# Output weights gated in a batch's second group, and the maxima's rows spread to the heads by a transfer

## What is computed

```python
mod = (silu(c) @ wmod).reshape(4, 6, 1, -1)          # sa, ca, ga, sb, cb, gb
ga = (2 * (ga >= 0) - 1) * maximum(abs(ga), 0.25)    # gb likewise
h = layernorm(x) * (1 + ca) + sa
q, k, v = split(h @ W_qkv.T); q, k = rope(q), rope(k)
y = softmax(causal(q @ k.T / sqrt(32))) @ v          # for each head
x = x + ga * (y @ W_o.T)
h = layernorm(x) * (1 + cb) + sb
x = x + gb * moe(h)      # top 2 of 16 by sigmoid(h @ Wg.T + bias), silu(h @ W1) @ W2
```

## Time and profile before

| | |
|---|---|
| median of three runs | 1663.24 us (1660.96 to 1666.24) |
| profiled execution | 1664.53 us, span 1662.6 us |
| TensorE (PE) busy | 1417.6 us, 85% |
| VectorE (DVE) busy | 1252.3 us, 75% |
| ScalarE (ACT) busy | 832.3 us, 50% |
| GpSimd (POOL) busy | 726.1 us, 44% |
| mean granted TensorE clock | 0.939 of full |

### The profile page before, as it was taken

One profiled execution on the slowest core, in us unless ns is written; L12 is line 12 of the kernel. 1 busy time (PEld: TensorE's weight loads), 2 busy tenths in 40 slices (PEclk: granted clock), 3 DMA queues, 4 the chain that ended last, 5 costly groups with the idle time before them and its releaser, 6 DMA issues. The chain is left out here.

```text
span 1662.6 us, 27877 instructions
## 1 busy us (share of the span) xinstructions
PE 1417.6 (85%) x8713; PEld 1008.2 (61%) x8713; DVE 1252.3 (75%) x2928; ACT 832.3 (50%) x1414; POOL 726.1 (44%) x683
## 2 busy tenths in 40 slices
PE   5579998799999889999988999999783999999900
PEld 3556665566566556656655565664341899999800
DVE  3578788687778868777886777888658677777778
ACT  4324557534454753445466434546323566666622
POOL 3244445342434534243443424344524677777500
PEclk9899999999999999999999999999885999999955
DMA  6644453544344353434445353434654555445389
GB/s 218 173 152 153 134 146 89 165 121 153 101 134 137 99 165 120 153 102 133 126 109 165 114 159 94 123 94 140 214 176 154 164 173 182 158 148 169 120 324 370
DMA packets 130098, 254.56 MB, mean 153 GB/s; under 512 B 15792, under 2 KB 67504, under 8 KB 129984
## 3 DMA queue, kind: packets, MB, share of 16 engines
q1 hardware_dynamic: 101888, 177.12, 34.5%
q0 software_dynamic: 13792, 47.72, 8.5%
q10 hardware_dynamic: 14304, 28.32, 5.1%
HBM read 167.34 MB, written 85.75 MB: 152 GB/s over the span
## 5 line engine op out<-in xcount | busy, mean ns | idle before, releaser
L674 ACT ACTIVATE probs<-ring 128x1024 f32<-128x1024 f32 (+3 forms) x384 | 310.2, 811 | 191.6 <-PE ring L528 115.8
L493 PE MATMUL ring<-stack_t 96*128 96x512 f32 (+3 forms) x768 | 296.6, 410 | 26.7 <-DMA stack_t<-stack_dram 23.5
L471 PE MATMUL ring<-w_parts,h_hi 128*128 128x384 f32 x1024 | 273.8, 349 | 9.2 <-DVE neg_max L855 4.0
L858 DVE CUSTOM_DVE_ANT_0 ring<-ring,later_b 128x384 f32<-128x384 f32 (+3 forms) x512 | 247.7, 496 | 31.5 <-PE ring L493 30.3
L493 PEld LDWEIGHTS ring<-stack_t 96*128 96x128 f32 x768 | 141.8, 193 | 181.5 <-issue 66.6
L1155 POOL TENSOR_TENSOR rope_a<-rope_a,rope_b 128x256 f32<-128x256 f32 x128 | 93.2, 728 | 348.6 <-DVE rope_b L928 348.5
L1142 POOL TENSOR_TENSOR prob_sum<-prob_sum,probs 128x1024 f32<-128x1024 f32 (+3 forms) x128 | 226.1, 1766 | 28.8 <-ACT probs L674 27.7
L522 PE MATMUL ring<-stack_t 128*128 128x512 f32 (+3 forms) x768 | 212.0, 358 | 23.0 <-ACT probs L674 11.2
L471 PEld LDWEIGHTS ring<-w_parts,h_hi 128*128 128x128 f32 x1024 | 188.9, 195 | 17.9 <-issue 12.9
L855 DVE TENSOR_REDUCE neg_max<-ring 128x1 f32<-128x512 f32 x256 | 174.9, 683 | 24.8 <-PE ring L493 22.6
L471 PE MATMUL ring<-w_parts,h_lo 128*128 128x384 f32 x512 | 176.2, 344 | 0.0
(11 more groups left out here) (192 smaller groups left out, 2439.3 us busy)
## 6 DMA issues: line engine op xcount, KB each, us to landing
stack_t<-stack_dram SPq DMA_DIRECT2D x384, 128.0 KB, 3.3
stack_dram<-parts SPq DMA_DIRECT2D x64, 512.0 KB, 2.7
w_parts<-w_dram SPq DMA_DIRECT2D x24, 768.0 KB, 6.6
w_sb<-y_dram SPq DMA_DIRECT2D x32, 512.0 KB, 6.7
w_sb<-w SPq DMA_DIRECT2D x22, 512.0 KB, 5.9
x_in<-x SPq DMA_DIRECT2D x32, 256.0 KB, 3.6
x<-x SPq DMA_DIRECT2D x32, 256.0 KB, 3.6
x_dram<-x SPq DMA_DIRECT2D x32, 256.0 KB, 2.4
```

The source lines that it names most:

```text
L471: mm = nc.tensor.matmul(ring[:, BANK[use], 0:384], lhs[:, c, cols], rhs[:, c, :], start=(k == 0), stop=(k == len(products) - 1))
L493: nc.tensor.matmul(ring[:, BANK[use], 0:width], stack_t[0:MROW, i % 2, 0, h, qt * P:qt * P + P], stack_t[0:MROW, i % 2, 1, h, kc * 512:kc ...
L674: nc.scalar.activation(probs[:, step % PROBS, :, q0:QC], ring[:, bank:bank + 2, q0:QC], ACT.Exp)\
L858: nc.vector.tensor_tensor_reduce(ring[:, BANK[use], 0:width], ring[:, BANK[use], 0:width], later_b[:, QC - width:QC], -1.0, 3e38, ALU.add, ...
```

## The change

The reads of the gate row and of the output weights move from steps 0 to 5 of the fourth group to steps 10 to 13 of the second group of the same batch; the modulation rows from step 7 of the fourth to step 15 of the second; the four products on POOL from steps 7, 8, 9, 11 of the fourth to steps 17, 19, 21, 23 of the second. ScalarE copies the maxima's rows for head 0 alone; SyncE waits for that copy and issues a transfer within SBUF from head 0's rows to those of heads 1 to 3, and TensorE waits for the transfer. Besides, two pairs of semaphores on POOL are merged into one each.

```diff
-LOAD_MOD2 = {STEPS * (G * b + G - 1): b for b in range(B)}
-LOAD_W_OUT = {step + 2 + n: (b, n) for step, b in LOAD_MOD2.items() for n in range(G)}
-LOAD_MOD_ROWS = {step + 7: b for step, b in LOAD_MOD2.items()}
-GATE_OUT = {step + at: (b, n) for step, b in LOAD_MOD2.items() for n, at in enumerate((7, 8, 9, 11))}
+LOAD_MOD2 = {STEPS * (G * b + 1) + 10: b for b in range(B)}
+LOAD_W_OUT = {step + n: (b, n) for step, b in LOAD_MOD2.items() for n in range(G)}
+LOAD_MOD_ROWS = {step + 5: b for step, b in LOAD_MOD2.items()}
+GATE_OUT = {step + at: (b, n) for step, b in LOAD_MOD2.items() for n, at in enumerate((7, 9, 11, 13))}
...
+            rows_in = [sem("rows_in0"), sem("rows_in1")]
...
+                    def rows_to_heads(i, half):
+                        rows = stack_t[MROW:MROW + 2 * HG, i % 2, 0, :, half * QC:half * QC + QC].bitcast(f32)
+                        sp.wait_ge(max_in, 2 * i + half + 1)
+                        sp.dma_start(rows[:, 1:HG, :], rows[:, 0:1, :].to_broadcast([2 * HG, HG - 1, QC]))\
+                            .then_inc(rows_in[half], 16)
...
                         if step in STACK_IN:
                             stack_parts(*STACK_IN[step])
+                        if step in MAX_TURN:
+                            rows_to_heads(*MAX_TURN[step])
                         if step in SECOND_STAT:
...
                         if kt == 0 and hp == 0:
-                            pe.wait_ge(max_in, 2 * i + qc + 1)
+                            pe.wait_ge(rows_in[qc], 16 * (i + 1))
...
-                        nc.scalar.copy(stack_t[MROW:MROW + 2 * HG, i % 2, 0, :, half * QC:half * QC + QC],
-                                       row.unsqueeze(1).to_broadcast([2 * HG, HG, QC])).then_inc(max_in, 1)
+                        nc.scalar.copy(stack_t[MROW:MROW + 2 * HG, i % 2, 0, 0, half * QC:half * QC + QC], row)\
+                            .then_inc(max_in, 1)
...
-                            dve.wait_ge(rstd2_ready, u - 1)
+                            dve.wait_ge(rstd2_ready, 2 * (u - 1))
...
-                        dve.wait_ge(rstd2_ready, u + 1)
+                        dve.wait_ge(rstd2_ready, 2 * u + 2)
...
-                            .then_inc(rstd_pow, 1)
-                        pool.wait_ge(rstd_pow, u + 1)
+                            .then_inc(rstd_step, 1)
+                        pool.wait_ge(rstd_step, 2 * u + 2)
```

More of the change, by code:

```diff
@@ L297, in adaln_block @@
             x_in_s = [sem(f"x_in{k}") for k in range(3)]
-            stat_step, rstd_step, rstd_pow, rstd_ready = (
-                sem("stat_step"), sem("rstd_step"), sem("rstd_pow"), sem("rstd_ready"))
+            stat_step, rstd_step, rstd_ready = (
+                sem("stat_step"), sem("rstd_step"), sem("rstd_ready"))
             stat_ready, x_hat_ready, h_scaled = sem("stat_ready"), sem("x_hat_ready"), sem("h_scaled")
@@ L312, in adaln_block @@
             o_ps, x1_ready, res_in = sem("o_ps"), sem("x1_ready"), [sem("res_in0"), sem("res_in1")]
-            stat2_step, stat2_ready, rstd2_step, rstd2_ready = (
-                sem("stat2_step"), sem("stat2_ready"), sem("rstd2_step"), sem("rstd2_ready"))
+            stat2_step, stat2_ready, rstd2_ready = (
+                sem("stat2_step"), sem("stat2_ready"), sem("rstd2_ready"))
             x_hat2, h2_ready = sem("x_hat2"), sem("h2_ready")
@@ L1108, in first_deviation @@
                             .then_inc(rstd_step, 1)
-                        pool.wait_ge(rstd_step, u + 1)
+                        pool.wait_ge(rstd_step, 2 * u + 1)
                         nc.gpsimd.tensor_tensor(rstd[:, u % 2, 1:2], rstd[:, u % 2, 0:1], neg_half[:, :], ALU.pow)\
-                            .then_inc(rstd_pow, 1)
-                        pool.wait_ge(rstd_pow, u + 1)
+                            .then_inc(rstd_step, 1)
+                        pool.wait_ge(rstd_step, 2 * u + 2)
                         nc.gpsimd.tensor_scalar(rstd[:, u % 2, 2:3], mean_var[:, u % 2, 0:1], rstd[:, u % 2, 1:2], -1.0,
@@ L1119, in second_deviation @@
                         nc.gpsimd.tensor_scalar(rstd2[:, u % 2, 0:1], mean_var2[:, u % 2, 1:2], EPS, None, ALU.add)\
-                            .then_inc(rstd2_step, 1)
-                        pool.wait_ge(rstd2_step, u + 1)
+                            .then_inc(rstd2_ready, 1)
+                        pool.wait_ge(rstd2_ready, 2 * u + 1)
                         nc.gpsimd.tensor_tensor(rstd2[:, u % 2, 1:2], rstd2[:, u % 2, 0:1], neg_half[:, :], ALU.pow)\
```

## The result

The changed kernel takes 1652.32 us (median of four runs, 1650.18 to 1653.38) against 1662.37 us for the kernel before, measured beside it: a ratio of 0.9934, 95% interval 0.9914 to 0.9955. A second set of runs, further down, gives 0.9928 (0.9910 to 0.9945). The gain is real, but 10 to 13 us where 27 were forecast; the median lies just above the upper end of the range, 1652. The profiled execution took 1653.06 us, span 1650.1 us.

What follows compares the result with a forecast made beforehand. The prediction took the attention part to be bound by TensorE nearly everywhere, with gains only where it waits or runs at half clock. 10.0 + 13.8 + 4.2 - 1.0 = 27.0 us gave a median of about 1636 us, range 1628 to 1652.

Steps and rivals of the forecast that it cites:

- (a): Last batch: early gated weights remove TensorE's wait before the output projection and its half clock; gain 10.0 us.
- R4: Rival: the residual holds the last batch's projection instead, so no gain there; 1646 us, chance 0.08.
- (b): Fourth groups, batches 0 to 2: TensorE's waits for stacked q/k parts and the half clock behind go; gain 13.8 us.
- R1: Rival: the third pair's stack in the fourth groups stays late; 1650 us, chance 0.17.
- (c): Second groups: the reads and POOL products moved there cost zero, at most 1 us for each batch.
- part 1: Output weights read and gated early, in the second group: gains of 10.0 and 13.8 us.
- small things: Allowance of 1 us for possible small costs, such as the row transfer and delayed expert loads in the last group.
- Part 2: Maxima's rows copied for one head: 1.28 us of ScalarE saved 32 times, worth 4.2 us on the path.
- The four places: Step 3 of three fourth groups and the last group, where the shorter copy saves TensorE waiting: 4.2 us.
- The transfer: SyncE's row transfer, taken to land in 2.7 us: cost 0, up to 5 us in the last group.
- R2: Rival: the row transfer on SyncE's queue delays the stacked parts in 15 groups; 1700 us, chance 0.04.

Runs made afterwards that it cites:

- e5: Changed kernel with four-head row copies, no row transfer, and early output weights in the last batch only: 1649.33 us, ratio 0.9928.
- e1: Changed kernel with only the early weight reads and gating; rows copied for all four heads, no transfer: 1642.42 us, ratio 0.9867.
- e6: Changed kernel with four-head row copies, no transfer, and early output weights in batches 0 to 2 only: 1653.25 us, ratio 0.9940.
- e7: Kernel before with only the two modulation rows read early, at step 15 of the second group: 1654.94 us, ratio 0.9956.
- e11: e5 with the modulation rows of all batches also read in the second group: 1643.33 us, ratio 0.9884.
- e4: Changed kernel with the copy for all four heads put back and the row transfer kept: 1642.09 us, ratio 0.9859.
- e3: Changed kernel with VectorE's probability sum waiting for POOL's reciprocal root in steps with a layer norm: 1639.01 us, ratio 0.9846.
- e9: Changed kernel, unaltered, measured again against the kernel before: 1650.48 us, ratio 0.9928.
- e12: e3 measured once more, beside e10: 1641.82 us, ratio 0.9873.
- e8: e2 with VectorE's sum also waiting for POOL's reciprocal root, as in e3: 1655.23 us, ratio 0.9959.
- e10: e1 with VectorE's sum also waiting for POOL's reciprocal root, as in e3: 1641.35 us, ratio 0.9869.
- e2: Changed kernel with output weights and modulation rows at their old steps; one-head copy and transfer kept: 1665.28 us, ratio 1.0005.

## Why the forecast was right and wrong

**(a) The last batch: right.** From the copy of step 2 to the output projection it was 1182.79 - 1160.23 = 22.56 us before and is 1170.43 - 1156.53 = 13.90 after: 8.7 us; the projection itself is 1.96 us shorter. Together 10.6 us, where 10.0 and the copy's 1.3 were forecast. By their ratios e5 gives 12 us for it, and e1 less e6 also 12. Nothing else held the projection's place, so R4 did not come.

**(b) The stacked parts: mechanism right, size too large.** The waits went, as did the half clock behind them, and the fourth groups are 78.5 us each, as forecast (near 78). The half clock itself was misread: in steps of 1 us the trace before shows it for 6.8, 3.4 and 6.8 us behind the three waits, not for about 4 us each, so 8.5 us of full clock were lost there and not 5.7. But the changed kernel still has 3.4 us of half clock in each of its fourth groups, at another place (below), so that 3.4 us of the 8.5 came back. In the profile on record the fourth groups lost 15.0 us with the copy's share in it (15.9 were forecast). But the runs give 7 to 10 us for it (e7, e6). A part of the gap is that the term was read from one execution: in the third profile of the kernel before the fourth groups are 7.5 us shorter, so that only 7.5 of the 15.0 us were there to be won; in batch 2 of that profile the modulation rows left 2.4 us behind the stack and there was no wait. The rest is open: two of three profiles show the full waits, and what the slower executions of e7 paid instead no profile of mine shows. Of the DMAs to which the forecast gave the blame, the modulation rows were the ones (e7); the weight reads were innocent (e11). R1, which had the stack stay late, gave 1650 us, near the result, but by a mechanism that did not occur.

**(c) The second group: right.** 229.2 against 227.3 us for four, 0.5 us each; forecast "at most 1 us for each batch". One of the four, batch 2's with 57.8 us, lies just above the 57.5 of the forecast.

Together part 1 is worth 22 us (interval 18 to 26), and the forecast had 23.8 less 1 for small things.

**Part 2: this step failed.** The forecast put the copies at a gain of 4.2 us and gave the bounds "0 and 1.86 us each", as if a shorter instruction could not cost. Measured against e1 or e4, the shorter copy costs 8 to 10 us. The two spans of e1 and of the changed kernel differ by 12.7 us: third groups 5.8, fourth 2.3, first 1.4, the last group up to its projection 1.1, 2.3 behind that, and next to nothing in the others together. The held operation itself is the smaller part of this. Third groups that have equally much half clock in them are about 1.1 us longer with it (batch 1, 3.4 us of half clock: 73.6 to 74.0 us in three profiles after 72.5 to 72.8 in nine; batch 2, 6.8 us: 75.9 to 76.0 after 74.8 and 74.9), some 3.3 us for three. The rest goes with half clock: three third groups hold 10 to 17 us of it in the three profiles with the turned order, and 0 to 14 in the thirteen others. The longer waits may make it likelier, but the same short waits are followed by half clock in one profile and not in another, and two profiles can't tell how much of it hangs on the turned order; e3, which differs by the one wait, is 12.9 us shorter than the changed kernel, and e9, which doesn't differ, 5.5. The medians tell more: the one wait brings back the whole 8 to 10 us (e3, e12; 10 us in e8), so over many executions the half clock goes with the order as well.

The four places at which the copy was to be on the path paid less than forecast. In the fourth group of batch 1 the wait of 0.71 us became 0.26, and 1.03 us of waiting two steps on, which was there before and after, now has half clock behind it:

```profile
601.62 0.47 PE L531 MATMUL ring<-stack_t 128*128 128x256 f32 x2 [0.26 <-ACT probs L683]
...
606.20 0.58 PE L480 MATMUL ring<-w_parts,h_hi 128*128 128x384 f32 x2 [1.03 <-DVE neg_max L867]
...
604.00:608.00 4.00, 2.81 (x13) 2.54 (x14) 3.86 (x13) 0.88 (x3) 0.79 (x2) 0.86 0.00 0
```

In the last group TensorE's wait behind the copy went from 1.55 us to 0.48, but the stall in front of the row of 1165.20 us grew from 1.60 to 2.20. With the order put right, fourth groups with the short copy are 77.5 or 78.5 us and with the long one 77.8: as far as these runs can tell, the term was 0 and not 4.2 (e10 and e12).

**The transfer.** It costs nothing (e4), and R2 did not come. Its landing was taken as 2.7 us from the earlier trace rows; beside the expert loads it is 5.2 us in e8, nearer to the upper bound of the text, and TensorE waits 0.2 us for it in e2 and 0.9 in e8. The estimate of 2.9 us by the Trainium skill ("SBUF — State Buffer") is too low beside these loads in the same way; no run here shows the transfer's time without them.

In sum: forecast 10.0 + 13.8 + 4.2 - 1.0 = 27.0; by the runs about 12 + 10 - 10 = 12.

## What to carry over

Making an instruction shorter moves everything behind it, and where two engines can hold each other up, a few tenths of a microsecond decide which one is held: before giving a saving the lower bound of nothing, look for the pair of operations that it brings together and ask who waits for each. If the wrong one is held, an explicit wait that fixes the order can be worth more than the saving. And a wait for a DMA that is a few microseconds late differs between executions, so take a second profile before it goes into a sum at full size.

## What the hardware showed

- The last operation of the root, one element in each partition, takes 0.26 us alone and 1.34 us when it starts 0.07 us before VectorE's sum of two SBUF buffers; the sum takes 1.22 us when it goes through and 2.92 to 3.4 us when POOL's sum of 2.4 us is ahead of it. The operation was held although it had started first by the records, in nine cases of nine.
- A wait of TensorE of 1.0 us was followed by a full clock before (264.28 us) and one of 1.70 us by half clock after; elsewhere one of 1.03 us was followed by half clock (606.20 us). The same wait of 1.03 us in e9, the same kernel, was followed by full clock, and the group is 77.5 us instead of 78.5. Each first group of batches 1 to 3, in all profiles here, is 79.5 to 79.8 or 81.1 to 81.2 us long, with nothing between.
- Two reads of 256 KB, issued 1.8 us behind the first of six transfers of 128 KB, made the slowest of these land after 8.4 us; in the changed kernel it is 3.6 us. Over 18 such pairs TensorE waited 1.65 to 4.11 us where the reads were issued 1.3 to 1.8 us behind that first transfer, and at most 0.78 us where it was 2.4 to 2.9 us.
